# Attention in a fused kernel: a new order of blocks on TensorE, position tables as the stationary operand, and row terms, column terms and the maximum on VectorE in fewer passes

## The chip, the cores and the metric

One core of one Trainium2 chip. The metric is the device time of the whole kernel in microseconds (us); the smaller the better.

## The reference

Four layers over x of 4 images of 16 by 16 positions and 1024 channels, each as x = x + layer(group_norm(x)). Layer 0 is a lambda layer, layer 3 a factorised convolution; the change doesn't touch their computation. Layers 1 and 2 are attention with 16 heads of 64 channels over 256 positions. Layer 1 has a causal mask in half of the heads and an anticausal one in the others. Layer 2 has biases and adds decomposed relative positions to the scores:

```python
qkv = hidden_states @ qkv_w + qkv_b
attn = jnp.einsum('bqc,bkc->bqk', q * scale, k)
rel_h = jnp.einsum('bhwc,hkc->bhwk', rq, Rh)
rel_w = jnp.einsum('bhwc,wkc->bhwk', rq, Rw)
attn = attn + rel_h[:, :, :, :, None] + rel_w[:, :, :, None, :]
attn = jax.nn.softmax(attn, axis=-1)
out = (attn @ v) @ proj_w + proj_b
```

## The kernel before

Channels lie on the 128 partitions in 8 chunks, tokens along the free dimension. Every float32 operand of a projection is split into a high and a low part (fp32r), and a product is three matmuls: high by high, low by high, high by low. Weights come in half blocks (slots) of 128 by 512 numbers: SP loads them (line 212), GpSimd (POOL) splits them (lines 226, 228), into three buffers in turn, so that a slot is split when PE has done the one three before it. The order of the slots is written by hand (take_block, lines 172 to 192) and must be PE's.

The two attention layers are worked off in 4 stages (layer 1 or 2, first or second pair of images) of 8 items; an item i is a pair of heads on two images, with j = i % 8. The items 0 to 15 are layer 1, the items 16 to 31 layer 2. For each item there are blocks K, Q and V (24 matmuls of 512 columns each, project, line 1142), scores (24 matmuls, line 1183), attention (attend, lines 1216 and 1227), and in layer 2 the products of q with the position tables (relative, line 1247: q is stationary, the tables of 64 columns stream). After a stage's last item come 8 output blocks (out_block); they stand in the next stage's item with j = 0. The last stage's output blocks close the attention, mixed with 16 small products of the last layer's matrix (build_m, line 1280).

PE's order in one item (lines 1304 to 1322) is: scores(i), relative(i+1), K(i+1), attend(i-1), V(i), a quarter of Q(i+2), the transposes of v(i) (turn_values, line 1197), the rest of Q(i+2). PSUM banks: scores in 2 to 5, K in 1, V in 0, attention in 6, Q and relative in 7.

The softmax goes to and fro between VectorE (DVE) and ScalarE (ACT), for the four quarters k of an item: maxima (DVE, lines 1475 and 1478, in layer 2 lines 1482 and 1485), exps (ACT, line 1373), invert_sums (DVE, 1500), normalize (ACT, 1383), turn_probs (DVE, 32 by 32 transposes, 1496). The probabilities go to DRAM and back to be turned (SP, lines 1649, 1656), in slots given by PROBS_AT; attend waits for them. In layer 2 the products of relative go from PSUM through ACT (1407) to DRAM (strips_to_dram) and come back skewed (strips_from_dram, 1638) as a row term and a column term per query; DVE sums the two over all keys (sum_relative, 1539: two SBUF inputs), and line 1482 adds the sum to the scaled scores.

An item's other steps: evac_q and rest_of_q (high and low part of q, lines 1393 or 1397 on ACT and 1513 or 1515 on DVE), evac_k and rest_of_k (1416 or 1418, and 1522 or 1524), evac_o and rest_of_o (1427, 1544), evac_v (ACT, 1361 or 1363) before and take_v (DVE, 1506) after the transposes of v. For j = 1 to 4 an item also normalises two chunks of the next stage's input: norm.y on both engines (406 on ACT, 408 on DVE), norm.head on ACT (414) and norm.rest on DVE (419, two SBUF inputs); at j = 0 DVE adds the output blocks (1551, 1553) and takes their statistics (373, 379, 325 to 337). Each engine runs its instructions in the order of the code: for ACT that is lines 1432 to 1455, for DVE lines 1564 to 1608. In both, evac_q(i+1) and rest_of_q(i+1) stand first in item i.

Of the kernel before, what the change touches and what calls it, by code (L numbers as in the profile page):

```python
# [67 lines left out]
def build(nc, A, out):  # L68
    outer = ExitStack()
    with outer:  # L70
# [108 lines left out]
        for i in range(ITEMS):  # L179
            s, j = i // PAIRS, i % PAIRS  # L180
            if i + 1 < ITEMS:
                take_block(i + 1, "K")
            take_block(i, "V", range(0 if i else 1, 2))
            if s and j == 0:
                for o in range(CK):
                    take((s - 1, "O", o), STAGES[s - 1][0], "O", o)
            if i + 2 < ITEMS:
                take_block(i + 2, "Q")
            for o in {ITEMS - 2: (0,), ITEMS - 1: (1, 2)}.get(i, ()):
                take((3, "O", o), 2, "O", o, (0,))  # L190
        for o in range(CK):
            take((3, "O", o), 2, "O", o, (1,) if o < 3 else range(2))
# [534 lines left out]
def later_layers(nc, A, out, outer, g):  # L727
# [36 lines left out]
    both_rel = carve(12288, [P, 2, 2, SIDE, SIDE])  # L764
    v = carve(19968, [P, 4, P])
    vT = carve(13312, [P, HALF])
    prob = carve(13824, [P, 2, 2 * N])
    probB = [carve(at, [P, 4 * N]) for at in (14848, 11264)]
    rel = carve(15872, [P, 2, 64])
    rel_hi, rel_lo = (carve(16000 + P * i, [P, 2, 64], F32R) for i in range(2))  # L770
    all_rel = carve(19456, [P, 4, 2, 2, 32])
# [3 lines left out]
    turned = nc.dram_tensor("turned", (2, 2, P, 4 * N), F32).ap()  # L775
# [27 lines left out]
    v_evac = sem("v_evac")  # L803
    v_tr = sem("v_tr")
# [22 lines left out]
    rel_sum = sem("rel_sum")  # L827
# [279 lines left out]
    REL = (X, 0)  # L1107
# [7 lines left out]
    def turned_bank(i):  # L1115

        return X if i == LAST - 1 else S

    def out_bank(s, o):
        return (1, X, 0)[o % 3] if s == 3 else (O, 0)[o % 2]  # L1120


    M_AFTER = {(0, 1): (), (1, 1): (0, 1), (2, 1): (2, 3), (3, 0): (4,), (3, 1): (5, 6),
               (4, 0): (7,), (4, 1): (8, 9), (5, 0): (10, 11), (5, 1): (12,), (6, 0): (13,), (6, 1): (14,), (7, 0): (15,), (7, 1): ()}
# [4 lines left out]
    def attention_pe(pe):  # L1129
# [12 lines left out]
        def project(i, kind, chunks):  # L1142
# [3 lines left out]
            for c in chunks:  # L1146
# [3 lines left out]
                if c == 0 and kind == "Q" and i > 1:  # L1150
                    pe.wait_ge(q_hi, i)
                    pe.wait_ge(q_lo, i)
                    if i - 1 >= LO_KEYS:
                        pe.wait_ge(rel_evac, 2 * (i - 1 - LO_KEYS) + 2)
                if c == 0 and kind == "V" and i:
                    pe.wait_ge(v_evac, i)
                    if LO_KEYS <= i + 1 < ITEMS:
                        pe.wait_ge(rel_evac, 2 * (i + 1 - LO_KEYS) + 2)
# [8 lines left out]
        def scores(i, a):  # L1167
# [5 lines left out]
            if i:  # L1173
                pe.wait_ge(p_exp, 4 * (i - 1) + 2 * a + 2)
                if a == 0 and turned_bank(i - 1) == S:
                    pe.wait_ge(v_ready, i)
# [10 lines left out]

        def turn_values(i):
            pe.wait_ge(v_evac, i + 1)
            if turned_bank(i) == S:  # L1190
                pe.wait_ge(p_exp, 4 * i + 1)
            else:
                pe.wait_ge(rel_evac, 2 * (ITEMS - LO_KEYS))
            if i:
                pe.wait_ge(v_ready, i)
            for tt in range(4):
                m = nc.tensor.transpose(PS[:, turned_bank(i), tt * P:tt * P + P], vT[:, tt * P:tt * P + P], ident[:, :])  # L1197
            m.then_inc(v_tr, 1)
# [33 lines left out]
        def relative(i):  # L1232

            if i == ITEMS or layer_of(i) == 1:
# [3 lines left out]
            pe.wait_ge(v_evac, i - 1)  # L1238
            if i % PAIRS == 2:
                pe.wait_ge(sum_done, CK * (i // PAIRS))  # L1240
            pe.wait_ge(tables_ready, 1)
            for tt in range(4):
                for k, (x, y) in enumerate(((qh[i % 2], rel_hi), (qh[i % 2], rel_lo), (ql[i % 2], rel_hi))):
                    for hh in range(2):
                        rows = slice(64 * hh, 64 * hh + 64)
                        to = PS[:, REL[hh], 64 * tt:64 * tt + 64].rearrange("p (t n) -> p t n", t=2)
                        m = nc.tensor.matmul(to, x[rows, tt * P:tt * P + P], y[rows, :, 32 * hh:32 * hh + 32],  # L1247
                                             start=k == 0, stop=k == 2)
                        if (tt, k) == (3, 2):
                            m.then_inc(rel_done, 1)  # L1250

        def out_block(s, o, chunks):
            for c in chunks:
                beside = 3 if s == 3 else 2
# [5 lines left out]
                if c == 0 and s < 3 and o == 1:  # L1260
                    pe.wait_ge(v_evac, PAIRS * (s + 1) + 1)
# [6 lines left out]
                if s == 3 and c == 0 and o == 1:  # L1268
                    pe.wait_ge(v_ready, LAST)
                if s == 3 and c == 0 and o == 2:  # L1270
                    pe.wait_ge(v_evac, ITEMS)
                chunk_of((s, "O", o), c, lambda hl, c: (oh, ol)[hl][:, c, :], out_bank(s, o))

        def build_m(i):
            if i % 4 == 0:
                pe.wait_ge(bd_ready, i // 4 + 1)
            if i >= 2:
                pe.wait_ge(m_lo, i - 1)
            for s in range(2):
                m = nc.tensor.matmul(PS[:, PT + i % 2, s * 256:s * 256 + 256], BD[(i // 4) % 2][:, (2 * i + s) % 8, :],  # L1280
# [3 lines left out]
        def score_block(i):  # L1284

            scores(i, 0)
            scores(i, 1)
            relative(i + 1)
# [10 lines left out]
        project(1, "K", range(CK))  # L1299
        project(0, "V", range(4, CK))  # L1300
        project(2, "Q", range(0, 2))
        turn_values(0)
        project(2, "Q", range(2, CK))
        for i in range(1, LAST - 1):
            score_block(i)
            project(i + 1, "K", range(CK))
            attend(i - 1, 0)
            attend(i - 1, 1)
            project(i, "V", range(CK))
            if i % PAIRS == 0:  # L1310
                s = i // PAIRS - 1
                out_block(s, 0, range(CK))
                out_block(s, 1, range(0, 2))
                turn_values(i)
                out_block(s, 1, range(2, CK))
                for o in range(2, CK):
                    out_block(s, o, range(CK))
                project(i + 2, "Q", range(CK))
            else:
                project(i + 2, "Q", range(0, 2))  # L1320
                turn_values(i)
                project(i + 2, "Q", range(2, CK))
        i = LAST - 1
        score_block(i)
        project(LAST, "K", range(CK))
        attend(i - 1, 0)
        attend(i - 1, 1)
        project(i, "V", range(CK))
        scores(LAST, 0)
        scores(LAST, 1)  # L1330
        out_block(3, 0, range(0, 2))
        turn_values(i)
        out_block(3, 0, range(2, 4))
        project(LAST, "V", range(CK))
        attend(i, 0)
        attend(i, 1)
        out_block(3, 1, range(0, 4))
        turn_values(LAST)
        out_block(3, 2, range(0, 4))
        for o in range(3):  # L1340
            out_block(3, o, range(4, 7))
        attend(LAST, 0)
        attend(LAST, 1)
        for o in range(3):
            out_block(3, o, range(7, CK))
            for k in M_AFTER[o, 1]:
                build_m(k)
        for o in range(3, CK):
# [5 lines left out]
    def attention_act(act):  # L1354
        def evac_v(i):
            product_done(act, (i, "V"))
            if i:
                act.wait_ge(v_tr, i)
            src = PS[:, bank_of(i, "V"), :]
            if layer_of(i) == 1:  # L1360
                ins = nc.scalar.activation(vT, src, ACT.Copy)
            else:
                ins = nc.scalar.activation(vT, src, ACT.Identity, bias=bias[:, 16 + i % PAIRS:17 + i % PAIRS])
            ins.then_inc(v_evac, 1)

        def exps(i, k):
            n = 4 * i + k
            act.wait_ge(p_max, n + 1)
            if n >= 2:
                act.wait_ge(t_done, n - 1)  # L1370
            for qt, (lo, hi) in enumerate(spans(i)):
                at = prob_at(i, qt)
                last = nc.scalar.activation(prob[:, n % 2, at:at + hi - lo], PS[:, S + k, qt * N + lo:qt * N + hi],  # L1373
# [659 lines left out]
```

## Time and profile before

| | us |
|---|---|
| median of 3 runs | 1245.13 (1244.61 to 1247.14) |
| the profiled execution | 1246.36 |
| its span, first to last instruction | 1244.4 |
| PE busy | 1216.4 (98%) |
| DVE busy | 690.4 (55%) |
| ACT busy | 475.1 (38%) |
| POOL busy | 641.5 (52%) |

The first 250 us are layer 0, 250 to 660 the two stages of layer 1, 660 to 1130 those of layer 2, and the rest is layer 3. A PE row's mean duration contains the time through the array; what a matmul costs is the spacing from one to the next, which the chain shows.

### The profile page before, as it was taken

The page shows a single profiled execution, that of the slowest core. Times are in us where ns is not written, and L with a number is a line of the kernel's source. Part 1 is how long each engine was busy: PE and PEld are TensorE (multiplying, and loading weights), DVE is VectorE, ACT ScalarE, POOL GpSimd, SP SyncE. Part 2 cuts the span into 40 slices and gives each one's busy share as a digit, 9 for nine tenths or more (in the row PEclk, how much of TensorE's full clock was granted, in tenths as well). Part 3 has the DMA queues.
Part 4 walks back from the last instruction along what each step waited for, and adds up shares of the span by engine and source line. Part 5 has one row for each costly group of instructions (what it writes and reads, how often), then busy time and mean ns, then how long its engine had stood idle before and what let it go on. Part 6 is the DMA issues. An engine that isn't in the chain of part 4 may idle for free.

```text
span 1244.4 us, 19555 instructions
## 1 busy us (share of the span) xinstructions
PE 1216.4 (98%) x6768; PEld 975.0 (78%) x6768; DVE 690.4 (55%) x1434; ACT 475.1 (38%) x1229; POOL 641.5 (52%) x726
## 2 busy tenths in 40 slices
PE   6999999999999999999999999999999999889998
PEld 4788896478888888888888878777887787668887
DVE  7534444775665433666452578756347776476212
ACT  3611141034645320656341164644206555243212
POOL 4633389256565567555546655555665556464000
PEclk9999999999999999999999999999999999999999
DMA  5211124025564643454645356557535565620012
GB/s 185 84 46 48 34 56 117 8 65 160 154 169 137 184 134 97 127 177 128 185 136 166 86 160 212 180 160 223 168 102 151 175 209 156 205 60 1 29 40 68
DMA packets 129376, 155.03 MB, mean 125 GB/s; under 512 B 30080, under 2 KB 84000, under 8 KB 129280
## 3 DMA queue, kind: packets, MB, share of 16 engines
q1 hardware_dynamic: 118976, 146.92, 39.7%
q10 hardware_dynamic: 10304, 6.88, 1.8%
q8 instruction: 54, 0.88, 0.3%
q14 instruction: 42, 0.34, 0.1%
HBM read 111.81 MB, written 37.75 MB: 120 GB/s over the span
## 4 chain that ended last, share of the span: by engine, by line
PE 89%; DVE 5%; ACT 2%; issue 1%; DMA 1%; SPq 1%; POOL 0%; ACTq 0%; DVEq 0%; POOLq 0%
PE PS L1137 53%; PE PS L682 7%; PE PS L1758 7%; PE PS L1183 4%; PE PS L960 3%; PE PS L969 2%; PE PS L975 2%; PE PS L1227 2%; PE PS L1216 2%; PE PS L1775 2%; PE PS L1247 2%; PE PS L665 1%; PE PS L1197 1%; DVE bst L257 1%; PE PS L700 1%
## 5 line engine op out<-in xcount | busy, mean ns | idle before, releaser
L1137 PE MATMUL PS<-XB,w_hi 128*128 128x512 f32 x1024 | 340.5, 397 | 1.2 <-POOL w_lo L228 1.2
L226 POOL CAST w_hi<-w_raw 128x512 fp32r<-128x512 f32 x195 | 124.2, 637 | 307.5 <-PE PS L1137 213.0
L228 POOL TENSOR_TENSOR w_lo<-w_raw,w_hi 128x512 fp32r<-128x512 f32 x195 | 256.1, 1313 | 15.6
L1137 PEld LDWEIGHTS PS<-XB,w_hi 128*128 128x128 f32 x1024 | 192.2, 188 | 47.1 <-issue 5.0
L1137 PE MATMUL PS<-XB,w_lo 128*128 128x512 f32 x512 | 200.2, 391 | 0.0
L1137 PE MATMUL PS<-XB,part 128*128 128x512 f32 x768 | 190.3, 394 | 0.0
L1137 PEld LDWEIGHTS PS<-XB,part 128*128 128x128 f32 x768 | 141.9, 188 | 32.2 <-issue 2.3
L1373 ACT ACTIVATE part<-PS,nmax 128x256 f32<-128x256 f32 (+1 forms) x256 | 112.2, 443 | 141.6 <-DVE nmax L1485 93.2
L1383 ACT ACTIVATE part<-part,prec 128x256 f32<-128x256 f32 (+1 forms) x256 | 105.8, 476 | 27.7 <-DVE prec L1500 27.7
L228 POOL TENSOR_TENSOR part<-part,part 128x512 fp32r<-128x512 f32 x85 | 111.5, 1312 | 6.8
L1137 PE MATMUL PS<-part,w_hi 128*128 128x512 f32 x344 | 112.9, 395 | 1.5 <-DVE part L1544 1.5
L226 POOL CAST part<-part 128x512 fp32r<-128x512 f32 x85 | 54.1, 636 | 116.3 <-PE PS L1137 103.7
L1137 PEld LDWEIGHTS PS<-XB,w_lo 128*128 128x128 f32 x512 | 96.2, 188 | 18.5 <-issue 0.2
L1496 DVE STREAM_TRANSPOSE part<-part 128x384 f32<-128x384 f32 (+1 forms) x128 | 82.1, 641 | 49.9 <-ACT part L1383 49.9
L1137 PEld LDWEIGHTS PS<-part,w_hi 128*128 128x128 f32 x344 | 65.2, 190 | 15.9 <-ACT part L1427 1.9
L682 PE MATMUL PS<-XB,w_hi 128*128 128x512 f32 x256 | 70.9, 392 | 0.0
L1137 PE MATMUL PS<-part,w_lo 128*128 128x512 f32 x172 | 67.6, 393 | 0.0
L1397 ACT ACTIVATE part<-PS,bias 128x512 fp32r<-128x512 f32 x16 | 11.0, 688 | 143.1 <-PE PS L1137 143.1
L1506 DVE COPY part<-PS 128x512 f32<-128x512 f32 x32 | 22.1, 692 | 78.2 <-PE PS L1197 78.2
L1137 PE MATMUL PS<-part,part 128*128 128x512 f32 x252 | 62.9, 399 | 0.2 <-issue 0.2
L1539 DVE TENSOR_TENSOR part<-part 128x512 f32<-128x512 f32 x64 | 59.4, 947 | 0.0
L598 DVE COPY part<-PS 64x512 f32<-64x512 f32 x32 | 34.6, 1080 | 44.2 <-PE PS L700 43.9
(136 smaller groups left out, 1884.0 us busy)
## 6 DMA issues: line engine op xcount, KB each, us to landing
w_raw<-in_w SPq DMA_DIRECT2D x187, 256.0 KB, 2.8
part<-in_w SPq DMA_DIRECT2D x85, 256.0 KB, 2.8
turned<-part SPq DMA_DIRECT2D x128, 128.0 KB, 2.9
part<-turned SPq DMA_DIRECT2D x32, 512.0 KB, 5.0
turned<-part SPq DMA_DIRECT2D x128, 96.0 KB, 2.5
part<-turned SPq DMA_DIRECT2D x32, 384.0 KB, 4.0
strips<-part ACTq DMA_DIRECT2D x16, 256.0 KB, 2.7
out_x<-xT SPq DMA_DIRECT2D x16, 256.0 KB, 2.1
```

Of the source, the lines that this page charges most:

```text
L226: pool.tensor_copy(hi, raw).then_inc(w_hi_done, 1)
L228: pool.tensor_tensor(lo, raw, hi.bitcast(F32), ALU.subtract).then_inc(w_ready, 1)
L598: last = nc.vector.tensor_copy(dst, src)
L682: m = nc.tensor.matmul(PS[:, 2 * (n % 2) + h, :], wt[:, (c % 4) * P:(c % 4) * P + P], x_part(hl, h, c), start=c == k == 0, stop=c == CK - ...
L960: m = nc.tensor.matmul(bank[0:rows * SIDE, (x - x0) * w:(x - x0) * w + w], table, Qs[:, jp, x * N + SIDE * y0:x * N + SIDE * y1], start=jp ...
L1137: m = nc.tensor.matmul(PS[:, bank, :], wt[:, (c % 4) * P:(c % 4) * P + P], rhs(hl, c), start=c == k == 0, stop=c == CK - 1 and k == 2)
L1183: m = nc.tensor.matmul(PS[:, S + 2 * a + hh, at + lo:at + hi], x[rows, qs], y[rows, cols], start=k == 0, stop=k == 2)
L1373: last = nc.scalar.activation(prob[:, n % 2, at:at + hi - lo], PS[:, S + k, qt * N + lo:qt * N + hi], ACT.Exp, bias=nmax[:, k, qt:qt + 1], ...
L1383: last = nc.scalar.activation(p, p, ACT.Copy, scale=prec[:, k, qt:qt + 1])
L1496: nc.vector.transpose(dst, src).then_inc(t_done, 1)
L1539: nc.vector.tensor_tensor(both_rel[:, n % 2, :, :, :], of_row, of_col, ALU.add).then_inc(rel_sum, 1)
L1758: m = nc.tensor.matmul(PS[:, bank, :], x3(hl, b, c, tt * P), w[:, c, half * HALF:half * HALF + HALF], start=c == k == 0, stop=c == CK - 1 ...
```

## The change

In words:
- PE's order in an item is now scores(i), K(i+1), Q(i+2), V(i), attend(i-1). relative(i+2) (not i+1) is cut into V(i) after its fifth chunk, 15 of 24 matmuls. With j = 0, attend(i-1) stands in front of V(i). The slots follow.
- relative has the tables as the stationary operand and q as the moving one: 3 matmuls of 512 columns in bank 7 in place of 24 of 64 columns. Its result has table entries on partitions, and DVE turns it in 32 by 32 blocks (turn_relative); four DMAs on ACT's queue write it to DRAM in pieces of 128 bytes.
- v is no more transposed by PE: DVE turns it in 32 by 32 blocks out of PSUM (turn_values), SP writes and reads it through DRAM (values_to_dram, values_from_dram), and ACT puts it in order (take_v). Its bias is added after the attention (evac_o, rest_of_o).
- sum_relative is gone. In layer 2 the row terms are added to the scores in their bank, and then one tensor_tensor_reduce for each half adds the column terms and takes the maximum. The tables are divided by SCALE first.
- evac_q(i+2), rest_of_q(i+2) and turn_relative(i+2) stand behind the group norm's steps, at the end of item i; evac_o and rest_of_o of i-2 stand at its start.
- The probabilities of an item go to DRAM in four DMAs, not eight.
- At the end six output blocks run their first halves before the last attention; they have banks 1, 7, 2, 3, 4 and 0.

The diff, cut to its core:

```diff
             if i + 1 < ITEMS:
                 take_block(i + 1, "K")
+            if i + 2 < ITEMS:
+                take_block(i + 2, "Q")
             take_block(i, "V", range(0 if i else 1, 2))
...
-            for tt in range(4):
-                for k, (x, y) in enumerate(((qh[i % 2], rel_hi), (qh[i % 2], rel_lo), (ql[i % 2], rel_hi))):
-                    for hh in range(2):
...
+            for k, (x, y) in enumerate(((rel_hi, qh[i % 2]), (rel_lo, qh[i % 2]), (rel_hi, ql[i % 2]))):
+                m = nc.tensor.matmul(PS[:, X, :], x.rearrange("p r n -> p (r n)"), y.rearrange("p (a y x) -> p y a x", a=2, y=SIDE),
+                                     start=k == 0, stop=k == 2)
+            m.then_inc(rel_done, 1)
...
+        def values_block(i):
+
+            project(i, "V", range(0, 5))
+            relative(i + 2)
+            project(i, "V", range(5, CK))
...
         for i in range(1, LAST - 1):
             score_block(i)
             project(i + 1, "K", range(CK))
-            attend(i - 1, 0)
-            attend(i - 1, 1)
-            project(i, "V", range(CK))
-            if i % PAIRS == 0:
+            project(i + 2, "Q", range(CK))
+            if i % PAIRS:
+                values_block(i)
+                attend(i - 1, 0)
+                attend(i - 1, 1)
+            else:
+                attend(i - 1, 0)
+                attend(i - 1, 1)
+                values_block(i)
                 s = i // PAIRS - 1
...
+        out_block(3, 0, range(0, 4))
         project(LAST, "V", range(CK))
+        for o in (1, 2):
+            out_block(3, o, range(0, 4))
         attend(i, 0)
         attend(i, 1)
...
+        for o in (3, 4, 5):
+            out_block(3, o, range(0, 4))
         attend(LAST, 0)
         attend(LAST, 1)
...
     def attention_act(act):
...
+        def take_v(i):
+
+            act.wait_ge(v_in, 16 * (i + 1))
             if i:
+                act.wait_ge(o_done, 2 * i)
+            dst = v.rearrange("p t (b c) -> p t b c", b=4)
+            nc.scalar.activation(dst, vB.rearrange("p (b t c) -> p t b c", b=4, t=4), ACT.Copy).then_inc(v_ready, 1)
...
             j, s = i % PAIRS, i // PAIRS
-            if i:
-                evac_q(i + 1)
+            if i >= 2 and j != 1:
+                evac_o(i - 2)
             exps(i, 0)
             exps(i, 1)
             normalize(i, 0)
             normalize(i, 1)
-            evac_relative(i + 1)
             exps(i, 2)
             normalize(i, 2)
+            if i == LAST:
+                take_v(i - 1)
             exps(i, 3)
...
             normalize(i, 3)
             evac_k(i + 1)
-            if j:
-                evac_o(i - 1)
-            evac_v(i)
+            if 0 < i < LAST:
+                take_v(i - 1)
             if 1 <= j <= 4:
                 for c in (2 * j - 2, 2 * j - 1):
                     norm.y(nc.scalar, s + 1, c)
                 for c in (2 * j - 2, 2 * j - 1):
                     norm.head(s + 1, c)
+            evac_q(i + 2)
+            if i and j == 0:
+                evac_o(i - 1)
+            if LO_KEYS <= i + 2 < ITEMS:
+                strips_to_dram(act, i + 2)
...
     def attention_dve(dve):
...
-                nc.vector.scalar_tensor_tensor(scores, scores, SCALE, both_rel[:, n % 2, :, :, :].rearrange("p a h w -> p (a h w)"),
-                                               ALU.mult, ALU.add).then_inc(rel_added, 1)
...
+                nc.vector.tensor_tensor(whole, whole, of_row, ALU.add).then_inc(rel_added, 1)
                 dve.wait_ge(rel_added, n - 4 * LO_KEYS + 1)
-                last = nc.vector.tensor_reduce(nmax[:, k, :], scores.rearrange("p (a n) -> p a n", a=2), AX, ALU.max, negate=True)
+                for qt in range(2):
+                    tile = whole[:, qt, :, :]
+                    of_key = of_col[:, qt, :].rearrange("p (h w) -> p h w", h=1).broadcast_to([P, SIDE, SIDE])
+                    last = nc.vector.tensor_tensor_reduce(tile, tile, of_key, -SCALE, 3.0e38, ALU.add, ALU.min,
+                                                          accum_out=nmax[:, k, qt:qt + 1])
...
+        def turn_values(i):
+
+            product_done(dve, (i, "V"))
             if i:
+                dve.wait_ge(v_ready, i)
+            src = PS[:, bank_of(i, "V"), :].rearrange("p (t q c) -> p t q c", t=4, q=4)
+            dst = vB.rearrange("p (q t c) -> p t q c", q=4, t=4)
+            nc.vector.transpose(dst, src).then_inc(v_turned, 1)
...
+            if i >= 2 and j != 1:
+                rest_of_o(i - 2)
             maxima(i, 0)
             maxima(i, 1)
...
             if i < LAST:
                 rest_of_k(i + 1)
-            if j:
+            if j == 1:
+                norm.coefficients(s + 1)
+            if 1 <= j <= 4:
+                for c in (2 * j - 2, 2 * j - 1):
+                    norm.y(nc.vector, s + 1, c)
+                for c in (2 * j - 2, 2 * j - 1):
+                    norm.rest(s + 1, c)
+            rest_of_q(i + 2)
+            if i and j == 0:
                 rest_of_o(i - 1)
-            if i and j == 0:
-                take_v(i)
+            turn_relative(i + 2)
+            if i < LAST:
+                turn_values(i)
...
+    STRIPS_AT = [slots[(i, "K"), 0] + (7 if i < LAST else 6) for i in range(ITEMS)]
+    PROBS_AT = [slots[(i + 1, "K"), 0] + 9 for i in range(LAST)] + [slots[(3, "O", 5), 0]]
+    BACK_AT = [PROBS_AT[i] + 2 for i in range(LAST - 1)] + [PROBS_AT[LAST - 1]]
```

## Rows read from the trace of the kernel before

**Rows 1.** The page, busy time by engine: busy us, share of the span, instructions.
```profile
PE 1216.4 (98%) x6768; PEld 975.0 (78%) x6768; DVE 690.4 (55%) x1434; ACT 475.1 (38%) x1229; POOL 641.5 (52%) x726
```
**Rows 2.** PE's waits: who waited for whom, us in total, times, longest.
```profile
PE PS L1280 <- DVE part L1731: 2.6, 3, 1.5
PE PS L1197 <- ACT part L1363: 2.6, 1, 2.6
PE PS L1216 <- DMA part<-turned: 2.3, 4, 1.1
PE PS L1137 <- DVE part L1544: 1.5, 1, 1.5
```
**Rows 3.** The chain, one item of layer 2: start us, us, what.
```profile
973.24 1.62 PE PS L1183 x24
974.86 1.52 PE PS L1247 x24
976.38 5.66 PE PS L1137 x24
...
990.95 0.44 PE PS L1197 x4
...
995.52 0.55 PE PS L1183 x5
```
**Rows 4.** The chain, one item of layer 1, from scores to scores.
```profile
597.49 1.52 PE PS L1183 x24
...
617.88 0.31 PE PS L1183
```
**Rows 5.** DVE in time, item with j = 3: start, us, line, operation [idle before].
```profile
751.12 0.75 DVE L1515 SCALAR_TENSOR_TENSOR part<-PS,bias,part 128x512 fp32r<-128x512 f32 x1 [0.51 <-ACT part L1397]
...
753.54 0.69 DVE L1482 SCALAR_TENSOR_TENSOR PS<-PS,part 128x512 f32<-128x512 f32 x1
...
760.74 1.08 DVE L1539 TENSOR_TENSOR part<-part 128x512 f32<-128x512 f32 x1
...
766.27 0.71 DVE L1524 SCALAR_TENSOR_TENSOR part<-PS,bias,part 128x512 fp32r<-128x512 f32 x1
...
770.33 2.56 DVE L419 TENSOR_TENSOR XB<-part,XB 128x512 fp32r<-128x512 f32 x2 [0.45 <-ACT XB L414]
```
**Rows 6.** ACT in time, the same item.
```profile
755.36 0.19 ACT L1373 ACTIVATION_READ_ACCUMULATOR part<-PS,nmax 128x1 f32 x1
755.46 0.47 ACT L1373 ACTIVATE part<-PS,nmax 128x256 f32<-128x256 f32 x1
...
765.51 0.67 ACT L1418 ACTIVATE part<-PS,bias 128x512 fp32r<-128x512 f32 x1
...
767.33 1.08 ACT L406 ACTIVATE part<-xT,coef 128x256 f32<-128x256 f32 x2
769.60 1.15 ACT L414 ACTIVATE XB<-part 128x512 fp32r<-128x512 f32 x2 [1.18 <-DVE part L408]
```
**Rows 7.** The chain, a long unbroken run of 512-column matmuls.
```profile
663.60 42.21 PE PS L1137 x186
```
**Rows 8.** PE in time, right behind its longest wait of the last stage.
```profile
1077.33 4.57 PE L1137 MATMUL PS<-part,part 128*128 128x512 f32 x12
```
**Rows 9.** The chain, the output block after the waits for line 1731.
```profile
1097.29 4.33 PE PS L1137 x12
```
**Rows 10.** DVE in time, layer 1: reductions over 256 and 128 scores.
```profile
583.06 0.62 DVE L1478 TENSOR_REDUCE nmax<-PS 128x1 f32<-128x256 f32 x2
```
**Rows 11.** Line 419 on DVE: durations in ns, least, median, most, first and last start.
```profile
L419 DVE TENSOR_TENSOR XB<-part,XB x40: 684/866/1777, 246.1 to 1016.1; 128x512 fp32r<-128x512 f32 x40
```
**Rows 12.** DVE in time, from the stage's last output sum to its statistics.
```profile
700.40 0.69 DVE L1551 TENSOR_TENSOR xT<-PS,xT 128x512 f32<-128x512 f32 x1 [4.09 <-PE PS L1137]
...
704.71 0.15 DVE L337 TENSOR_SCALAR gn<-gn 128x1 f32<-128x1 f32 x1
```
**Rows 13.** Windows: stretch, us, then PE, PEld, DVE, ACT, POOL busy, PEclk, DMA share, GB/s.
```profile
1077.30:1081.70 4.40, 4.40 (x15) 3.54 (x14) 0.69 (x1) 0.00 (x0) 0.00 (x0) 0.61 0.92 232
```

More of the change, by code:

```diff
@@ L1299, in attention_pe @@
         project(1, "K", range(CK))
+        project(2, "Q", range(CK))
         project(0, "V", range(4, CK))
-        project(2, "Q", range(0, 2))
-        turn_values(0)
-        project(2, "Q", range(2, CK))
         for i in range(1, LAST - 1):
@@ L1455, in attention_act @@
                     norm.head(s + 1, c)
+            evac_q(i + 2)
[3 more added lines that the diff above has]
+                strips_to_dram(act, i + 2)
+        evac_o(LAST - 1)
+        take_v(LAST)
         evac_o(LAST)
@@ L1581, in attention_dve @@
             turn_probs(i, 2)
-            if i and j == 0:
-                rest_of_o(i - 1)
+            if i == LAST:
+                turn_values(i)
             invert_sums(i, 3)
@@ L1599, in attention_dve @@
                 norm.group_stats(s + 1)
-            if j or i == 0:
-                take_v(i)
-            if j == 0:
-                norm.coefficients(s + 1)
-            if 1 <= j <= 4:
-                for c in (2 * j - 2, 2 * j - 1):
-                    norm.y(nc.vector, s + 1, c)
-                for c in (2 * j - 2, 2 * j - 1):
-                    norm.rest(s + 1, c)
+        rest_of_o(LAST - 1)
         rest_of_o(LAST)
         for o in range(CK):
-            for k in M_AFTER.get((o, 0), ()):
-                rest_of_m(dve, k)
+            if o >= 6:
+                for k in M_AFTER[o, 0]:
+                    rest_of_m(dve, k)
+                for k in (2 * o - 12, 2 * o - 11):
+                    stats_of(3, k)
             add_out(3, o)
-            if o:
-                stats_of(3, o - 1)
             for k in M_AFTER[o, 1]:
                 rest_of_m(dve, k)
-        stats_of(3, CK - 1)
+        for o in range(4, CK):
+            stats_of(3, o)
         norm.aggregate(5, range(CK), 16)
@@ L1623, in strips_to_dram @@
         buf, done = i % 2, i - LO_KEYS
-        sp.wait_ge(rel_evac, 2 * done + 2)
-        whole = strips[buf].rearrange("(t p) n -> p t n", p=P)
-        sp.dma_start(whole, all_rel[:, :, :, :, :].rearrange("p t a b n -> p t (a b n)")).then_inc(strips_out, 16)
+        sp.wait_ge(rel_evac, done + 1)
+        rows = strips[buf].rearrange("(ax y) n -> ax y n", y=SIDE)
+        for b in range(4):
+            src = all_rel[32 * b:32 * b + 32, :].rearrange("p (y n) -> p y n", y=SIDE)
+            sp.dma_start(rows[:, :, 32 * b:32 * b + 32], src).then_inc(strips_out, 16)
```

273 lines of the change are left out of this document (119 added, 154 removed).

## The prediction

> **What bounds the kernel now.** I read the engine shares first: TensorE (PE) is busy 98% of the span [rows 1]. So the time is PE's work plus PE's waits. The list of PE's waits [rows 2] holds, in the part that the change touches, four lines of 9.0 us. Then the chain, window by window, for one cycle: an item i (two heads) costs PE scores, the position products of i+1, a K block, the attention of i-1, a V block with the first quarter of a Q block, four transposes, and the rest of Q: 22.28 us from one scores to the next in the second attention layer, with 1.62 for scores, 1.52 for the position products, 5.66 for a block and 0.44 for the transposes [rows 3], and 20.39 without the position products in the first [rows 4]. There are no gaps in either. Last I read VectorE (DVE) and ScalarE (ACT) over such a cycle, that from 750.36 [rows 5, 6], to see how late each result is that PE will need after the change. Today the only result in a tight loop is k_lo, which line 1524 makes 15.91 us after the scores begin and PE wants at 22.3.
>
> **What PE saves.** The transposes of v leave PE: 32 items by 0.44 us [rows 3, 4] = 14.0. The position products were 24 matmuls of 64 columns in 1.52 us; they become 3 of 512 columns. A 512-column matmul follows the next after 5.66/24 = 0.236 us [rows 3], or 42.21/186 = 0.227 in a long run [rows 7], so 3 take 0.69: 16 items by 0.83 = 13.3. One restart fewer per item, 24 (0.236 - 0.227) = 0.2 at most and nothing at least, I put at 1.5 for all. In the last stage PE waits 8.5 us today, the four lines of the list less 0.5 in an earlier cycle, and after two of the waits it runs slow: 12 matmuls (2.7 us by the spacing) took 4.57 and 4.33 [rows 2, 8, 9]. That is 3.5 more, 12.0 in all. The new order puts six first halves of output blocks between scores(30) and the last attention; by my count the last probabilities land about when PE comes for them, so I keep 10.5 as the gain and leave 1.5 for waits on line 1280. Sum: 14.0 + 13.3 + 1.5 + 10.5 = 39.3 us less.
>
> **What the new order asks for.** relative(i+2) now stands after 15 matmuls of V(i), and needs q_lo(i+2). From the start of scores(i) PE arrives there after 1.62 + 5.66 + 5.45 + 3.41 = 16.14 us (scores, K with its restart, then 24 of Q and 15 of V at 0.227). Behind the waiting matmul stand the rest of V(i), the attention of i-1 and scores(i+1), which starts the next round of the same chain: a wait here isn't made up, it is paid in each cycle. In the old kernel evac_q was first in an item, right behind its Q block; now it is behind all of the item's softmax and, for j = 1 to 4, behind the group norm of the next stage, on both engines.
>
> I date q_lo(i+2) from rows. Today the old chain reaches rest_of_k (line 1524) 15.91 us after scores at 750.36 [rows 5]. The change takes the sums of row and column terms (line 1539) out of it: the first maxima start at 753.54, 3.18 after the scores; the new first step is evac_o and rest_of_o (0.76 until DVE starts, as line 1515 does after PE's last matmul, and 0.66 itself), so 1.42, 1.76 earlier. Of the later sums, one of 1.08 us (760.74) stands before the third reciprocal; by ACT's times the exponentials hid 0.6 of it, so 0.46 more: 13.69. It adds d to each of four maxima. One reduction of 512 elements becomes two fused passes over 256: a pass over 256 and one over 128 together span 0.62 [rows 10]; 128 more elements at the rate by which 0.69 us reads 512 (less 0.1 fixed) are 0.13, so two of 256 are 0.75 less what the next start overlaps, 0.66, against 0.61: +0.05. DVE's accumulator isn't in the trace. ACT's readout adds 0.10 to its activation (755.36 to 755.46) [rows 6], twice 0.10. So d lies between 0.05 and 0.25; if each fused pass took as long as a reduction of 512, d = 0.6. I take 0.2, since the ACT row is the nearest, and 4d = 0.8. rest_of_k is then at 14.5.
>
> By the Trainium skill, "VectorE: DVE Perf Modes", section "Two Vector instructions with no wait between them", a DVE instruction that writes its accumulator is two instructions. The ACT rows show that form; no row shows it on DVE. Without that rule the sum would take d = 0.05, some 0.6 us earlier in each cycle.
>
> - **j = 5, 6, 7** (and without norm). ACT is at evac_k at 765.51, so 12.93 + 0.8; take_v follows at 14.3 and evac_q at 14.9; rest_of_q 0.7 later, 0.75 long [rows 5, 6]: 16.4. PE waits 0.25; four cycles (21, 22, 23, 29) make 1.0.
> - **j = 2, 3, 4.** ACT's two y take 1.08 from 14.9 to 15.95, the head starts then, the rests 0.73 after it (769.60 to 770.33). Two rests took 2.56 in this cycle, and twice the median of all of them is 1.73 [rows 5, 11]. I take 1.8, as GpSimd has less to do while PE waits. Then rest_of_q, 0.75: 15.95 + 0.73 + 1.8 + 0.75 = 19.25. PE waits 3.1, six times: 18.6.
> - **j = 1** (items 17, 25). DVE comes from the stage's last sum and statistics: 700.40 to 704.86 [rows 12], and it starts as soon as PE's last output matmul is done; scores now follow that at once, so the maxima start at 4.5 and not 1.42, and rest_of_k at 17.6. Then 0.64 of its own, coefficients 0.6, the y 1.08, 0.73, two rests at their least 1.35, 0.75: 22.7. PE waits 6.5, twice: 13.0.
> - **j = 0 and item 30.** Attention of i-1 follows straight after two blocks, at 1.62 + 5.66 + 5.45 = 12.7, and needs take_v(i-1), which stands behind the softmax on ACT: 14.3 + 0.65 = 14.95. 2.2 us, three times (16, 24, 30): 6.6. In the first layer (item 8) the softmax is over near 11 us, so nothing.
>
> Sum of waits 39.2. Then the clock: the wait of 2.6 us by line 1197 was followed by 4.4 us at a mean granted clock of 0.61, thus mostly the lower of its two levels (1.2 and 2.4 GHz), and cost 1.8; the waits of line 1280 were followed by the like, 1.6 [rows 2, 8, 9, 13]. Eight waits of 3 us or more by about 1.0 (some of the slow stretch falls where the next cycle waits anyway), and three of 2.2 by 0.7: 10. Bounds 0 and 18.
>
> **Beside other work, at nothing.** SP issues 4 + 4 writes and 3 reads where it issued 8 + 2; attention comes a whole cycle later than its reads. ACT issues 4 strip writes instead of one, between its evac_q and the attention's end. DVE's turns of v and of the position products (no more than line 1515's 0.75 each) lie in the same pause. If the cover goes, each costs its own 0.6 per cycle.
>
> By the Trainium skill, "SBUF — State Buffer", section "Who interferes with whom", a DVE instruction with two SBUF inputs is slowed while GpSimd reads SBUF. Line 419 is such a one: 0.68 to 1.78 us [rows 11], so the trace agrees. With that and GpSimd splitting weights all the time the two rests would cost 2.5 and each wait 0.7 more.
>
> **The sum.** 39.3 saved, 39.2 + 10 lost: +10 on the profiled 1246.36 us (span 1244.4). The median shown is 1.2 lower, so 1255.
>
> **Rivals.**
> 1. *The new loop through q_lo costs more than PE saves* (my forecast, 0.58): +10, own range -2 to +30: 1243 to 1275, since each tenth of d is 0.4 us in some 14 cycles, rests 0.7, clock 0 to 18. Speaks for it: the order in the code, and that the same sum gives today's rest_of_k. It decides where q_lo passes 16.14 us.
> 2. *The loop holds off PE much less*, because ACT and DVE overlap more than I line up: waits of half size and no slow clock, -20: 1225; none at all, 1207. 0.24. For it: both engines stand idle for much of a cycle. Against: ACT's idle time in front of the first exponentials is spent waiting for DVE, and DVE's for ACT; the chain alternates between them and is as long as their sum.
> 3. *The fused pass is dear*: d = 0.6, so 1.6 us more in 14 cycles, with the clock +25 on my sum: 1280. 0.12. Nothing in the trace prices it.
> 4. *Both sides cancel*, within noise: 1245. 0.06.
>
> A measurement of this kernel can tell about 0.2% (2.5 us) from no change. Below 1242.6: all of rival 2 but a little, and the low edge of 1: 0.27. Within: rival 4 and a part of 1: 0.12. Above: 0.61. The range leaves out 2's lower half and the upper part of 3: 1222 to 1280; the likeliest case's own is 1243 to 1275.
>
> **What would show it.** PE waiting on DVE's rest_of_q before the three position matmuls: 3 us for j = 2 to 4, 6 for j = 1, near none for j = 5 to 7; cycles of the first attention layer at 19.9, of the second at 20.9 plus the wait; a granted clock under 1 after waits; the last stage 10 us shorter. It is wrong if those waits are under 1.5 us, if the fused pass is outside 0.3 to 0.5 us, or if a queue that I put at nothing (SP, the strips' small pieces) sets the end.

## The result, and the profile after

The changed kernel takes 1268.86 us (1267.62 to 1269.73), the kernel before 1245.59 (1244.61 to 1247.14) beside it: ratio 1.0192, 95% interval 1.0179 to 1.0204. It is slower by 23 us, where I had forecast 10 (1255); the time lies near the upper edge of the forecast's own range, 1243 to 1275. Its profiled execution took 1269.73 us, 23.4 more than that of before (1246.36).

The first lines of the page say that PE's work went down and the time up. Against [rows 1], PE has 464 instructions and 16.3 us of busy time fewer, in a span that is 23.5 longer; and in the strip of the granted clock the figures fall to 8 in two places, slices that cover 697 to 761 us and 951 to 1014 us; item 17 begins at 698 and item 25 at 941.

```profile
span 1267.9 us, 18684 instructions
...
PE 1200.1 (95%) x6304; PEld 961.9 (76%) x6304; DVE 656.9 (52%) x1578; ACT 464.6 (37%) x1197; POOL 632.6 (50%) x727
...
PEclk9999999999999999999999889999998899999999
```

PE's waits in the part that the change touches (who waited for whom, us in total, times, longest) were four lines of 9.0 us before [rows 2]. Now:

```profile
PE PS L1225 <- issue: 33.2, 9, 6.5
PE PS L1198 <- issue: 7.6, 2, 4.0
PE PS L1209 <- issue: 4.7, 1, 4.7
PE PS L1262 <- DVE part L1749: 2.0, 4, 0.6
PE PS L1225 <- ACT part L1373: 2.0, 1, 2.0
```

Line 1225 is relative, 1198 and 1209 the attention of the two layers, 1262 the last stage's build_m. PE in time (start, us, [idle before]) gives each wait its item: here are the three position matmuls that stand in items 17 (j = 1), 18, 21, 22 and 23, and the scores that follow the first three of them:

```profile
720.71 1.62 PE L1225 MATMUL PS<-part,part 128*128 128x512 f32 x3 [6.53 <-issue]
728.20 1.70 PE L1177 MATMUL PS<-part,part 64*128 64x256 f32 x24
747.72 1.62 PE L1225 MATMUL PS<-part,part 128*128 128x512 f32 x3 [3.32 <-issue]
755.35 1.70 PE L1177 MATMUL PS<-part,part 64*128 64x256 f32 x24
...
823.19 0.96 PE L1225 MATMUL PS<-part,part 128*128 128x512 f32 x3
828.02 1.69 PE L1177 MATMUL PS<-part,part 64*128 64x256 f32 x24
846.18 0.96 PE L1225 MATMUL PS<-part,part 128*128 128x512 f32 x3 [1.96 <-ACT part L1373]
...
867.76 0.96 PE L1225 MATMUL PS<-part,part 128*128 128x512 f32 x3 [0.52 <-issue]
```

The waits of 3.32 us come six times (j = 2 to 4), the second of j = 1 is 6.22. "issue" only says that the profile names no releaser. DVE in time names it: PE starts 0.1 us after rest_of_q (line 1499) ends, here in the items 17 and 18. The attention waits end in the same way, 0.1 us after take_v (line 1338 on ACT), here in item 30:

```profile
719.87 0.74 DVE L1499 SCALAR_TENSOR_TENSOR part<-PS,bias,part 128x512 fp32r<-128x512 f32 x1
746.88 0.74 DVE L1499 SCALAR_TENSOR_TENSOR part<-PS,bias,part 128x512 fp32r<-128x512 f32 x1
...
1086.44 0.62 ACT L1338 ACTIVATE part<-part 128x512 f32<-128x512 f32 x1
1087.16 2.52 PE L1198 MATMUL PS<-part,part 128*64 128x256 f32 x16 [3.97 <-issue]
```

The PE rows also show what the clock does. From relative to the next scores PE has the same work each time: 4.83 us where nothing was waited for (823.19 to 828.02), 7.49 and 7.63 behind the first two waits. In windows (stretch, us, PE busy, granted clock, DMA share, GB/s):

```profile
720.70:722.30 1.60, 1.59 (x4) 0.50 0.77 169
722.30:726.20 3.90, 3.90 (x12) 0.50 0.48 111
726.20:728.30 2.10, 2.10 (x18) 0.91 0.20 32
```

A clock of 0.50 is the lower of the two levels: here PE works at half speed for some 5.5 us after it stood still for 6.53.

The account of the 23.4 us, each part summed over the profiled execution of after:
- waits before relative: 6.53 + 6.22 + 6 x 3.32 + 1.96 + 0.52 = 35.2;
- waits before the attention at items 16, 24 and 30: 4.74 + 3.64 + 3.97 = 12.4;
- slow clock: the eight stretches from relative to scores last 7.49, 7.63, 6.17, 6.36, 7.37, 7.57, 6.10, 6.36, less 4.83 each = 16.4; 1.2 behind the wait of item 16 and 1.6 behind that of item 30: 19.2;
- together 66.8 lost, so the rest of the change saved 66.8 - 23.4 = 43.4. This last figure is what is left over, not a measurement of its own.

### The profile page after: what moved, and what is told of

Same layout as the page of the kernel before. It is cut to its first block, busy times and chain, and to the rows that moved or that the text cites. A ratio compares the mean times of both kernels' runs of the same rounds, so it can differ in the third digit from the quotient of the medians.

```text
span 1267.9 us, 18684 instructions
## 1 busy us (share of the span) xinstructions
PE 1200.1 (95%) x6304; PEld 961.9 (76%) x6304; DVE 656.9 (52%) x1578; ACT 464.6 (37%) x1197; POOL 632.6 (50%) x727
## 4 chain that ended last, share of the span: by engine, by line
PE 78%; DVE 7%; issue 6%; ACT 5%; POOL 1%; DMA 1%; ACTq 0%; SPq 0%; POOLq 0%; DVEq 0%
PE PS L1135 45%; PE PS L1776 7%; PE PS L682 7%; PE PS L960 3%; PE PS L1177 3%; PE PS L1198 2%; PE PS L969 2%; PE PS L975 2%; PE PS L1209 2%; ACT part L1349 2%; DVE PS L1460 2%; PE PS L1793 2%; PE PS L1225 1%; DVE PS L1465 1%; PE PS L665 1%
## 5 line engine op out<-in xcount | busy, mean ns | idle before, releaser
L226 POOL CAST w_hi<-w_raw 128x512 fp32r<-128x512 f32 x195 | 121.6, 623 | 322.3 <-PE PS L1135 246.6
L228 POOL TENSOR_TENSOR w_lo<-w_raw,w_hi 128x512 fp32r<-128x512 f32 x195 | 252.2, 1294 | 15.6
L1135 PEld LDWEIGHTS PS<-XB,w_hi 128*128 128x128 f32 x1024 | 195.0, 190 | 46.0 <-issue 2.2
L1135 PE MATMUL PS<-XB,part 128*128 128x512 f32 x768 | 192.9, 400 | 0.0
L1135 PEld LDWEIGHTS PS<-XB,part 128*128 128x128 f32 x768 | 147.6, 193 | 32.4
L1135 PEld LDWEIGHTS PS<-XB,w_lo 128*128 128x128 f32 x512 | 97.5, 190 | 20.1 <-issue 0.2
L1359 ACT ACTIVATE part<-part,prec 128x256 f32<-128x256 f32 (+1 forms) x256 | 105.8, 475 | 18.7 <-DVE prec L1481 18.7
L1490 DVE STREAM_TRANSPOSE part<-PS 128x512 f32<-128x512 f32 x32 | 22.9, 715 | 62.4 <-PE PS L1135 61.3
L682 PEld LDWEIGHTS PS<-XB,w_hi 128*128 128x128 f32 x256 | 47.4, 188 | 9.4
L1135 PEld LDWEIGHTS PS<-part,part 128*128 128x128 f32 x252 | 47.1, 188 | 9.7
```

Of the source, the lines that this page charges most:

```text
L226: pool.tensor_copy(hi, raw).then_inc(w_hi_done, 1)
L228: pool.tensor_tensor(lo, raw, hi.bitcast(F32), ALU.subtract).then_inc(w_ready, 1)
L682: m = nc.tensor.matmul(PS[:, 2 * (n % 2) + h, :], wt[:, (c % 4) * P:(c % 4) * P + P], x_part(hl, h, c), start=c == k == 0, stop=c == CK - ...
L1135: m = nc.tensor.matmul(PS[:, bank, :], wt[:, (c % 4) * P:(c % 4) * P + P], rhs(hl, c), start=c == k == 0, stop=c == CK - 1 and k == 2)
L1359: last = nc.scalar.activation(p, p, ACT.Copy, scale=prec[:, k, qt:qt + 1])
```

## The experiments

Line numbers in the text are those of the changed kernel; a row of an experiment has those of its own kernel, which can be some lines off. "ratio" is against the kernel before, with its 95% interval.

**Theory A**: PE is held by the chain of DVE and ACT that ends in q_lo, and by the slow clock behind each wait. **Theory B**: the four strip writes, their small pieces or SP's queue set the pace. The kernels e1 and e3 tell these apart; e2 and e4 test the attention waits and the slow clock of theory A.

### e1: q ahead of the group norm

```diff
+            evac_q(i + 2)
             if 1 <= j <= 4:
...
                 for c in (2 * j - 2, 2 * j - 1):
                     norm.head(s + 1, c)
-            evac_q(i + 2)
```

and on DVE rest_of_q(i + 2) likewise, ahead of the coefficients, norm.y and norm.rest.

> The changed kernel, with evac_q and rest_of_q of item i+2 ahead of the group norm's steps on both engines. Theory A (PE is held by the chain that ends in q_lo, and each wait of 3 us is followed by a slow stretch of some 2.6 us): at j = 2 to 4 the wait of 3.3 us falls to under 0.8 with no slow stretch, six times 5.3 = 32 us; at j = 1 the wait of 6.4 falls to about 3.4, twice 3 = 6 us: 1231 us. Theory B (the four strip writes, SP's queue or the many small pieces set the pace, and q_lo is only the place where it shows): the strips are written no earlier here, so at most a few us, over 1260.

1239.31 us, ratio 0.9958 (0.9946 to 0.9969). One swap of neighbours takes 29.6 us away, and the kernel is faster than the one before. So the norm's place alone cost more than the 23 us by which the change had made the kernel slower, and theory B, which allowed a few us, is out as the main cause. But 8 us of what theory A expected are missing. The waits did not go to zero: they come in every other cycle, at j = 3, 5 and 7, as here at j = 5 and j = 7, with j = 6 free:

```profile
809.22 1.62 PE L1225 MATMUL PS<-part,part 128*128 128x512 f32 x3 [2.62 <-ACT part L1373]
...
831.69 0.96 PE L1225 MATMUL PS<-part,part 128*128 128x512 f32 x3
...
854.49 0.95 PE L1225 MATMUL PS<-part,part 128*128 128x512 f32 x3 [1.74 <-ACT part L1373]
```

ACT in time, ahead of the item that ends in the wait of 2.62, shows why:

```profile
789.22 3.78 ACTq L1612 DMA_DIRECT2D strips<-part  x4
793.05 0.69 ACT L1395 ACTIVATE part<-PS,bias 128x512 fp32r<-128x512 f32 x1 [5.29 <-issue]
```

Scores(21) began at 790.41 and the item's evac_o could have begun with them; it began 2.64 later, behind ACT's own issue of four writes. Where PE had waited, the writes fit into the wait; where it had not, they start the next item late.

### e2: v taken early

```diff
             normalize(i, 2)
-            if i == LAST:
+            if i:
                 take_v(i - 1)
```

(and not behind evac_k any more)

> The changed kernel, with take_v of item i-1 ahead of the last exponentials on ACT, not behind evac_k. Theory A: the copy fits into ACT's idle 0.55 us there, attention no longer waits at items 16, 24 and 30 (12.4 us and some 3 of slow clock), and q_lo comes 0.5 us earlier in eight cycles: about 1250 us. Rival: v has not landed by then, or the copy delays the last exponentials by its 0.6 us, so that the chain grows by as much as it loses: 1262 or more, with the waits on q_lo as long as before.

1252.80 us, ratio 1.0070 (1.0043 to 1.0097): 16.1 less. The attention waits are down from 12.4 to 1.2, for which one of 1.8 stands before the last scores; the six of 3.32 fell to 3.13, not by the 0.5 I expected. Not all of the gain is fewer waits: in the profiled execution, 20.1 us shorter than that of the changed kernel, the eight stretches from relative to scores are 9.3 us too long and not 16.4, though the waits before them are nearly the same. Some 7 us of it are slow clock that happened to stay away, and the four runs spread over 6.4 us (1249.65 to 1256.05).

### e3: the strip writes on SP

```diff
-            if LO_KEYS <= i + 2 < ITEMS:
-                strips_to_dram(act, i + 2)
...
+                if i + 2 >= LO_KEYS and i + 2 < ITEMS and n == PROBS_AT[i] + 1:
+                    strips_to_dram(sp, i + 2)
```

> The changed kernel, with the four strip writes issued by SP (one weight slot behind the write of the probabilities) and not by ACT. Theory A: evac_o starts up to 1.9 us earlier in the items without a wait on q_lo, so the waits before relative at j = 5 to 7 (2.5 us) go and those of attention at items 16, 24, 30 shrink by 1.9 each; with a little clock 9 us less: 1260. Theory B (the writes on ACT's queue are the larger cause): waits shrink everywhere, under 1250. Rival C: SP, which also feeds the weights, becomes late, PE waits on w: slower than 1270.

1261.00 us, ratio 1.0143 (1.0118 to 1.0168): 7.9 less, near the 9 of theory A and far from B. ACT at item 30, first in the changed kernel, whose scores began at 1070.39:

```profile
1067.28 5.04 ACTq L1612 DMA_DIRECT2D strips<-part  x4
1072.37 0.69 ACT L1395 ACTIVATE part<-PS,bias 128x512 fp32r<-128x512 f32 x1 [7.72 <-issue]
```

and then in e3, with scores at 1061.97:

```profile
1062.09 0.69 ACT L1395 ACTIVATE part<-PS,bias 128x512 fp32r<-128x512 f32 x1 [5.86 <-PE PS L1198]
```

evac_o is 0.12 behind the scores, not 1.98. The attention waits are 2.82, 2.13 and 2.12, in sum 7.1 and not 12.4, and none is left at j = 5 to 7. Two new waits, 0.88 and 0.46 us, stand at the last attention; e1 and e2, whose writes are on ACT, have such waits too (0.84; 0.24 and 0.63), so they don't speak against SP's longer list, and no other wait of PE does.

### e4: work in place of the wait

```diff
+                for _ in range(27 if j == 1 else 14):
+                    nc.tensor.matmul(PS[:, O, :], rel_hi.rearrange("p r n -> p (r n)"), x_part(0, h, 0), start=True, stop=True)
             pe.wait_ge(q_hi, i + 1)
             pe.wait_ge(q_lo, i + 1)
```

> The changed kernel, with matmuls of 512 columns into the idle O bank, whose results nobody reads, ahead of the wait on q_lo: 14 at j = 2 to 4, 27 at j = 1, 138 in all or 31.3 us of added PE work where PE waits 32.7 us today. Nothing of the computation is left out. If the slow stretches follow from PE's standing idle and cost their full length (8 by 2.6 us): the added work makes the kernel faster by some 21 us, 1248. If they cost the 1.0 us each of my prediction: 1260. If the clock falls for another reason: 1268 to 1272.

1255.93 us, ratio 1.0096 (1.0069 to 1.0124). 138 matmuls more, and 12.9 us less. PE in time, for the same items 17 and 18:

```profile
720.99 0.96 PE L1231 MATMUL PS<-part,part 128*128 128x512 f32 x3 [0.50 <-DVE part L1505]
725.82 1.69 PE L1177 MATMUL PS<-part,part 64*128 64x256 f32 x24
745.41 0.96 PE L1231 MATMUL PS<-part,part 128*128 128x512 f32 x3 [0.23 <-DVE part L1505]
750.27 1.70 PE L1177 MATMUL PS<-part,part 64*128 64x256 f32 x24
```

In item 17 relative comes when it did (720.99 for 720.71), so the wait itself has only been filled; but the scores come 4.83 behind it and not 7.49. In the profile all eight stretches last 4.82 to 4.86: the 16.4 us are gone, some 1.7 come back in the attention of item 24, which here is slow. The difference of the two profiled executions is 14.9, as much as 16.4 less 1.7 gives (14.7). So the slow stretches come from PE's standing still, and cost their full length. That was the cause tested, and the size is between my 1.0 a wait (1260) and the 2.6 that I had read from the first two (1248): the mean of the eight is 2.05.

### e5, e7, e8: the edits together

e5 is the changed kernel with the edits of e1, e2 and e3, e7 with those of e1 and e3, e8 with those of e1 and e2.

> The changed kernel with all three edits: evac_q and rest_of_q ahead of the group norm, take_v ahead of the last exponentials, the strip writes on SP. Theory A (PE's waits and their slow stretches are the whole loss, and what PE saves is real): the order of q first gave 1239.3; take_v takes away the attention waits left there (3.4, 2.9, 2.6 and some clock: 12), the strips the waits of 1.7 to 2.6 us that came in every other cycle there (10): 1217. Rival: the edits gain on the same waits and SP becomes late: 1230 or more.

1222.66 us, ratio 0.9832 (0.9799 to 0.9865): 6 more than expected.

> Two of the edits: q first and the strip writes on SP, take_v where the change put it. Theory A: the waits in every other cycle of the kernel with q first alone (2.62, 1.74, 1.83, 2.06 us, on ACT's evac_q) come from ACT, which first issues four writes and only then takes o; with the writes gone they go, 10 to 12 us less than 1239.3: 1228. Rival (they come from the norm's steps, now last in the item, that delay the next item's start): waits stay, 1235 or more.

1224.39 us, ratio 0.9830 (0.9806 to 0.9855), below the 1228 expected: with q first and the writes on SP there is no wait before relative from j = 2 on, and a cycle is 21.1 us (742.66 to 763.81 and 763.81 to 784.92).

> Two of the edits: q first and take_v early, the strip writes still on ACT. Theory A: the attention waits (8.9 us and a little clock) go, q_lo comes 0.5 earlier, the waits in every other cycle stay: 1229. Rival: if the gains of the two edits are one and the same, 1237.

1226.63 us, ratio 0.9855 (0.9834 to 0.9876), near the 1229 expected; the waits left lie in most cycles now, 1.2 to 1.8 each.

So e5, with all three, brought hardly more than two of them (its four runs spread from 1221.14 to 1229.56, over both), and it had waits of 2.53, 1.79 and 1.98 us again that e7 does not have. ACT in e5 shows it:

```profile
751.43 0.63 ACT L1338 ACTIVATE part<-part 128x512 f32<-128x512 f32 x1 [2.88 <-DMA part<-values]
751.97 0.46 ACT L1349 ACTIVATE part<-PS,nmax 128x256 f32<-128x256 f32 x1
```

take_v stands ahead of the last exponentials, and v has not landed: SP issued its read at 746.47 (below), behind the other lists, and the copy could start only 4.96 later. The rest of the softmax waits behind it.

```profile
746.47 0.35 SPq L1656 DMA_DIRECT2D part<-values  x1
```

### e9: v early only where it is wanted

```diff
-            if i == LAST:
+            if i and (j == 0 or i >= LAST - 1):
                 take_v(i - 1)
```

on top of e7; in the items that take it here, take_v no longer stands behind evac_k.

> q first and the strip writes on SP, and take_v early only where attention needs v at once: at j = 0 and in the last items. In the kernel with all three edits ACT stood 2.88 us before its early copy, for v to land; the waits of 2 to 2.7 us before relative came from that. If so, those waits stay away here, the attention waits left in the kernel with two edits (2.8, 2.1, 2.1, with some 3 us of slow clock) go, one of 1.7 before the last scores comes: 1216 us. Rival (v lands too late at j = 0 too): 1223.

1217.07 us, ratio 0.9781 (0.9764 to 0.9798). This version beats both kernels: 28.4 us less than before, 51.8 less than the change as made. Its waits left:

```profile
PE PS L1225 <- ACT part L1373: 6.2, 2, 3.1
PE PS L1198 <- issue: 2.6, 2, 1.6
PE PS L1262 <- DVE part L1749: 2.0, 4, 0.6
PE PS L1177 <- DVE part L1506: 1.9, 1, 1.9
```

### e6: the fused instruction taken apart

```diff
-                    last = nc.vector.tensor_tensor_reduce(tile, tile, of_key, -SCALE, 3.0e38, ALU.add, ALU.min,
-                                                          accum_out=nmax[:, k, qt:qt + 1])
+                    nc.vector.scalar_tensor_tensor(tile, tile, SCALE, of_key, ALU.mult, ALU.add).then_inc(rel_added, 1)
+                last = nc.vector.tensor_reduce(nmax[:, k, :], scores.rearrange("p (a n) -> p a n", a=2), AX, ALU.max, negate=True)
```

on top of e5; the scale by which the exponentials read the scores moves with it, at no instruction more.

> All three edits, but the column terms and the maximum not in one instruction: per maxima two passes of 256 that add the columns, then the old reduction of 512 (0.69 us). Each maxima takes 0.7 us more, a cycle's four 2.8. Theory A (the chain of DVE and ACT up to q_lo sets when PE goes on): some 13 cycles wait 2.5 us each, with clock 30 to 50 us more than the kernel with all three edits. Rival (DVE has slack once q is first): within 5 us of it.

1255.21 us, ratio 1.0083 (1.0064 to 1.0102), 32.5 more than e5, from which it differs in this alone: slower even than the kernel before. DVE in time in e6, one maxima of 2.13 us:

```profile
745.98 0.69 DVE L1456 TENSOR_TENSOR PS<-PS,part 128x512 f32<-128x512 f32 x1
746.70 0.76 DVE L1461 SCALAR_TENSOR_TENSOR PS<-PS,part 128x256 f32<-128x256 f32 x2
747.50 0.69 DVE L1463 TENSOR_REDUCE nmax<-PS 128x2 f32<-128x512 f32 x1
748.11 0.69 DVE L1456 TENSOR_TENSOR PS<-PS,part 128x512 f32<-128x512 f32 x1
```

and in the changed kernel, 1.46 us:

```profile
782.54 0.69 DVE L1460 TENSOR_TENSOR PS<-PS,part 128x512 f32<-128x512 f32 x1
783.26 0.43 DVE L1465 CUSTOM_DVE_ANT_1 PS<-PS,part 128x256 f32<-128x256 f32 x1
783.62 0.14 DVE L1465 DVE_READ_ACCUMULATOR2_ANT nmax<- 128x1 f32 x1
783.62 0.47 DVE L1465 CUSTOM_DVE_ANT_1 PS<-PS,part 128x256 f32<-128x256 f32 x1
784.00 0.14 DVE L1465 DVE_READ_ACCUMULATOR2_ANT nmax<- 128x1 f32 x1
784.00 0.73 DVE L1460 TENSOR_TENSOR PS<-PS,part 128x512 f32<-128x512 f32 x1
```

0.67 us four times, 2.7 a cycle, and PE then waits 2.15 in every cycle from j = 2 on (5.2 at j = 1), with a slow stretch behind about half of them. So against the three passes it is a gain of its own, as large as the whole distance between the kernel before and the mended ones.

### e10, e11: relative moved on PE

e10 is built on e9, e11 on the changed kernel.

> The same, and at j = 1 relative(i+2) behind the attention of i-1 (3.9 us of PE work later), with DVE's turn of v ahead of its turn of the products. The two waits of 3.1 us there and their slow stretches of about 2.6 go: 11 us less than that kernel, 1205. Rival (the late turn delays DVE's next maxima by as much, and the wait comes back at j = 2): 1212 or more.

1218.64 us, ratio 0.9798 (0.9779 to 0.9816): no gain over e9, the rival was right. The wait of 3.09 at j = 1 has gone and one of 3.06 stands at j = 2:

```profile
712.01 0.99 PE L1225 MATMUL PS<-part,part 128*128 128x512 f32 x3
...
732.19 1.62 PE L1225 MATMUL PS<-part,part 128*128 128x512 f32 x3 [3.06 <-ACT part L1376]
```

> The changed kernel with one edit in PE's order: relative(i+2) behind the attention of i-1 in all cycles of j = 1 to 7, 3.9 us of PE work later, and DVE's turn of v ahead of that of the products; the group norm stays ahead of q. Rival (the wait is one of place alone): the waits of 3.3 go, those of 6.4 shrink to 2.5, with the slow stretches 45 us less: 1224. Theory A with the writes: ACT issues the four strip writes only after the turn, now at the end of the cycle, so evac_o and the next item's maxima start some 4 us late and q_lo with them: waits of about 3 us stay, 1252.

1256.34 us, ratio 1.0088 (1.0063 to 1.0113), so some 12 us won of the 45 of the rival. PE's waits before relative shrink from 35.2 to 16.2, but 23.4 stand before the attention where 12.4 stood: 6.81, 6.30 and 6.39 at the items 16, 24 and 30, and small ones in the others. The wait isn't one of place: PE is held by the length of the chain, and given a later place it meets the chain at a later step. That the strip writes, now at the end of the cycle, make up the difference is only argued; no run has e11 with the writes on SP.

## Why the prediction was wrong

The direction and the mechanism (rival 1) held, and the time is inside the range given for it. The size did not hold: 23 us and not 10. Two terms of the sum were too small, the strip writes on ACT, put at nothing, and the slow clock, cut to about half. Point by point, forecast against after:

**What PE saves**: 39.3 forecast, 43.4 by the account, 4 more. The first layer alone saved 12.0 us up to scores(16) (639.84 to 627.83), where my terms give 7.8; a cycle fell from 20.39 [rows 4] to 19.68 and not to 19.9. The row of the transposes, 0.44, was less than what they cost with their surroundings, 0.71; how that divides was not tried. In the second layer a free cycle is 21.1 and not 20.9: from the V matmul before the three 512-column matmuls to the one after them they add about 1.05 and not 0.69 (758.47 to 759.75 in e7, less one spacing). From scores(16) to scores(30), its waits and slow stretches taken off, the change saved 18.7, where the forecast leaves 21.0 (39.3 less 7.8 and 10.5). The last stage, from scores(30) to the end of the output blocks, fell by 7.1; item 30's wait of 4.0 and the 1.6 of slow clock behind it are in that, and without them it fell by 12.7, where I had 10.5. So the sum of the savings, 4 off, hides errors of both signs.

**The waits before relative**: 32.6 forecast, 35.2 measured. j = 2 to 4: 3.1 forecast, 3.32 measured. j = 1: 6.5, and 6.53 and 6.22. The dating of the chain from rows of the kernel before came out within 0.2 us at j = 2 to 4, and in that is luck: seen from the scores of item 19, the two rests of the group norm began 0.3 earlier than I had them and took 2.26 and not 1.8, as they do within 0.02 in all six cycles. The saving from "GpSimd has less to do while PE waits" was put too high; my dear case of 2.5 was nearer. For d, 0.2 was forecast for a maxima and 0.13 measured: 1.46 in the changed kernel against 1.33 before, from 753.54 [rows 5] to the next one's start:

```profile
754.87 0.69 DVE L1482 SCALAR_TENSOR_TENSOR PS<-PS,part 128x512 f32<-128x512 f32 x1
```

and in the changed kernel the rests of item 18:

```profile
744.62 2.33 DVE L419 TENSOR_TENSOR XB<-part,XB 128x512 fp32r<-128x512 f32 x2 [0.68 <-ACT XB L414]
```

By the Trainium skill, "VectorE: DVE Perf Modes", section "Two Vector instructions with no wait between them", a DVE instruction that also writes out its accumulator is two. The trace agrees, with a second row of 0.14 us each time; but the next instruction starts with that row and not behind it, so the readout costs nearly nothing here.

**The waits of the attention**: 6.6 forecast, 12.4 measured. The step that failed is "ACT issues 4 strip writes instead of one", which stood among the things put "at nothing". Their cover was PE's wait on q_lo; at j = 0 and in item 30 the item before had little or none, and the issue pushes evac_o, by 1.9 us in item 30, and with it the whole softmax. e3 takes them off ACT and finds 7.1, my 6.6. The same step was wrong by 1.5 us at j = 5 to 7 (2.5 measured, 1.0 forecast, none in e3). So my own sign, a queue put at nothing that sets the end, came true in these cycles. By the Trainium skill, "Perfetto Trace Analysis", section "What "DMA-bound" means", the slices on an issuing engine's own queue are the making of descriptors and not data on the way. The row above (5.04 us for four writes of 64 KB, and 2.60 in item 19) and e3 agree with that: the queue's time is taken from ACT.

**The clock**: 10 forecast, 19.2 measured. The step that failed is "by about 1.0 (some of the slow stretch falls where the next cycle waits anyway)". It doesn't: e4 took the eight stretches away and got all of them back. The likely reason is that the next wait is set by a chain that itself starts with the late scores, so the slow stretch moves everything behind it. I had 1.6 and 1.8 in my own rows [rows 2, 8, 9, 13] and cut them by an overlap that a closed loop can't have. At 1.8 for eight waits and 1.5 for three the term would have been 19; that it meets the 19.2 is partly luck, since the eight cost 2.05 on average and the three 1.2, nothing and 1.6.

The sum: waits 8.4 too small, clock 9.2 too small, savings 4.1 too small: 8.4 + 9.2 - 4.1 = 13.5, the distance from +10 to +23.4. That it closes proves nothing, since the savings are what the account leaves over; the waits and the stretches are read from rows, and e3 and e4 test them.

The rivals: 2 (engines overlap more than lined up) fell by the six equal waits of 3.32; 3 (the fused pass dear) by its rows, 0.43 and 0.47 us. That the parts themselves were good, and their order alone bad, I had not listed at all: with one swap, one list on another queue and one copy earlier the same parts make 1217.

## What to carry over

Behind a result that the matrix engine waits for in a closed loop, nothing may stand in its engines' queues that isn't needed as soon; look at what the change puts ahead of it, DMA issues too, and not only at what it removes. Count the slow clock behind such waits in full, with the size that the rows show. An issue list that is free while its engine waits for a slow loop stops being free once the loop is mended.

## What the runs showed of the hardware

- The slow stretch behind a wait is not a function of its length. Waits of 3.32 us in the changed kernel were followed by a stretch 1.3, 1.5, 2.7 or 2.8 us longer; in e2, two waits of 3.13 and 3.14 by none at all (the first: 975.27 to 980.09, 4.82; the stretch takes 4.83 where nothing is waited for), and in e10 the wait of 3.06 by 2.74. The same wait may start the slow clock at once (relative in 1.62) or later (0.95, then slow).

```profile
975.27 0.96 PE L1225 MATMUL PS<-part,part 128*128 128x512 f32 x3 [3.13 <-issue]
980.09 1.69 PE L1177 MATMUL PS<-part,part 64*128 64x256 f32 x24
```

- Adding 31 us of matmuls that fill PE's idle time made the kernel 12.9 us faster (e4).
- Four DMA writes of 64 KB in pieces of 128 bytes held ACT's queue for 2.60 to 5.04 us in the changed kernel, and SP's for 2.64 to 3.35 in e5.
